# A ring of 24 row slots for the first expert layer, and a combination that fetches two row blocks a step

## The chip, the cores and the metric

The kernel runs on one core of a Trainium2 chip. Time is device microseconds (us) of the whole launch. TensorE multiplies matrices (PE in the profile), VectorE is DVE, ScalarE is ACT, GpSimd is POOL, and SyncE (SP) only issues transfers. Each engine works through a list of its own in order and waits on semaphores for the others. "DMA" is a transfer; an indirect one gathers or scatters rows by a list of indices, and is issued from POOL's list here.

## The reference

Input x is 8 batches of 512 tokens with 128 values. Four layers follow, each added to x and each behind a layer norm: a linear one with a cumulative sum, a mixture of experts, local attention, and the same mixture of experts again. The experts:

```python
xn = (x - mu) * rsqrt(var + EPS) * gamma + beta
probs = softmax(einsum('btd,ed->bte', xn, router_w) / TEMP)
w, idx = top_k(probs, 2)                 # 2 of E = 8 experts per token
h = silu(einsum('btd,edf->betf', xn, W1))
y = einsum('betf,efd->betd', h, W2)
out = einsum('bte,betd->btd', wdense, y) # the two chosen experts, weighted
return out + res
```

The attention has 16 heads of 8 values; a query sees itself and the 128 tokens before it.

## The kernel before, in words

**Tiles of an expert layer.** Tokens are sorted by expert, so that each tile of 128 row slots has one expert; there are 71 tiles. A router works out for each slot which token it holds (`idx`) and where each token's two results lie (`posi`). It does so in two halves of four batches: the tiles below FIRST = 25 need the first half alone, tile 25 and all later ones the second half too. The normalised rows lie in DRAM as `table`. POOL fetches the 128 rows of a tile into a slot of `xg` (L502), TensorE transposes them (L1180, `xbank`), ScalarE scales them (L973, L974), VectorE forms the low part of `xT` (L829), TensorE multiplies by W1 (L1198 to L1200), ScalarE applies silu (L980), TensorE multiplies by W2 (L1208), VectorE copies the result into one of eight slots of `ysb` (L825), and in the first layer SP stores it to `yslot` (L332). In the second layer POOL scatters it to `ytab` (L509).

**Steps.** `layer_pass` lets every engine go through the same steps s. In step s TensorE transposes tile s, multiplies tile s - 2 by W1 and tile s - 4 by W2; VectorE copies the result of tile s - 5 first and then makes `xT` of tile s. The product of tile i by W2 waits until the results up to tile i - 2 are copied. POOL fetches tile s + 3. It may do so when the tile four before it has been transposed, since `xg` has G = 4 slots. In the first layer steps 4 to 21 also hold the router of the second half (`r_step`), and steps 0 to 7 the linear layer of batches 4 to 7 (`a_step`), whose norms need a rsqrt guess from POOL (`pow_`, L465). Steps 24 to 35 each hold one of 12 memsets of POOL (L492) that zero the space `qz` for the attention.

**What lies beside the tiles.** From step BESIDE_AT = 44 on, when the first 40 tiles (all that batches 0 to 3 need) are through, `beside` adds other work of the first layer at the end of a step. Its own count starts at 0 in step 44. POOL gathers the results of batches 0 to 3 back from `yslot` (L522), eight gathers of 128 rows for a batch, one a step from count 2 on. Each waits until the tile under way (s - 3) has passed W1. VectorE adds them to x (`combine`, L846), batch b at counts 11 + 8b and 12 + 8b, when all eight have landed. Then come the fronts of batches 0 and 1, which prepare their attention: statistics on VectorE (L575 to L584), a rsqrt guess on POOL, which stands behind that step's fetch and gather, normalising on VectorE (L604), transposes and the products for q, k and v on TensorE (L1092, L1229 to L1241), a dump of q and k to DRAM and their stacks back into `qz` and `kst` by SP (L373). FRONT_AT = 12 sets where batch 0's front starts, batch 1's comes 8 counts later. When the pass is over, TensorE issues four warming products (L1356) and the scores of batch 0 (L1267, L1272), which wait for its stacks and alternate with reductions of VectorE (L889).

**The space that the change uses.** `pT` holds exponentials in the attention alone: 128 partitions by 3072 values, as much as 24 slots of 128.

## Time and profile before

| | us |
|---|---|
| median of 3 runs | 809.58 |
| lowest, highest | 806.76, 812.36 |
| the profiled execution | 813.83 |
| its span (first to last instruction) | 812.1 |
| busy: TensorE, VectorE, ScalarE, POOL | 664.5, 455.8, 421.8, 331.7 |
| first expert layer: tile 0's transpose to the last W2 product | 73.5 to 267.2 |
| second expert layer: the same | from 598.7 |

An engine's busy time is a sum over stages that are bound by different things, so it has to be read beside the timeline of the stretch in question. "idle before <-releaser" in a row tells what ended an engine's wait; "issue" there means that it waited for nothing that the profile shows.

### The profile page before, as it was taken

What the parts mean: (1) busy time and instruction counts of PE and PEld (TensorE: products, weight loads), DVE (VectorE), ACT (ScalarE), POOL (GpSimd) and SP (SyncE); (2) the same over time, 40 slices, a digit from 0 to 9 for tenths busy, and PEclk for the clock granted to TensorE, in tenths of its full rate; (3) what the DMA queues carried; (4) which work ended last, traced back from release to release, by engine and by line L of the source; (5) the groups of instructions that cost most, each with busy time, mean ns of one, the idle gap of its engine ahead of it and who ended that gap; (6) DMA issues with size and microseconds to landing.
All of it is one profiled execution on the core that took longest, in us unless ns stands there. A gap on an engine that the chain in (4) does not pass through costs nothing.

```text
span 812.1 us, 29237 instructions
## 1 busy us (share of the span) xinstructions
PE 664.5 (82%) x11190; PEld 516.6 (64%) x11190; DVE 455.8 (56%) x1700; ACT 421.8 (52%) x804; POOL 331.7 (41%) x352
## 2 busy tenths in 40 slices
PE   4942988999989788989898988779669799888890
PEld 2521686888878447566665656556448687777680
DVE  7866768522345666575666665573865842224334
ACT  3442375666655047464565657355548465555440
POOL 4303442585777101131212100110056677777771
PEclk9985799999999679899999999797878999999996
DMA  7500031222334301121120201010012111214425
GB/s 225 146 9 17 21 91 44 56 68 73 83 75 116 118 17 60 36 67 50 56 79 20 83 17 58 15 41 6 3 33 73 43 53 51 53 53 116 130 67 165
DMA packets 61029, 52.57 MB, mean 65 GB/s; under 512 B 9729, under 2 KB 54402, under 8 KB 60890
## 3 DMA queue, kind: packets, MB, share of 16 engines
q1 hardware_dynamic: 52034, 32.54, 13.6%
q0 software_dynamic: 8864, 18.17, 8.5%
q8 instruction: 96, 1.57, 0.8%
q14 instruction: 35, 0.29, 0.1%
HBM read 30.74 MB, written 19.92 MB: 62 GB/s over the span
## 4 chain that ended last, share of the span: by engine, by line
PE 47%; DVE 19%; issue 10%; POOL 7%; DMA 7%; ACT 4%; DVEq 4%; SPq 1%; PEld 1%; PEldq 0%; POOLq 0%; ACTq 0%
PE stbank L1208 10%; PE bank L1314 4%; DMA xg<-table,idx 4%; PE stbank L1198 3%; PE sbank L1272 3%; POOL ytab L509 3%; PE sbank L1267 3%; PE stbank L1298 3%; PE stbank L1200 2%; POOL xg L502 2%; DVE mx L889 2%; PE stbank L1199 2%; PE bank L1092 2%; DVE zr L604 2%; PE sbank L1180 1%
## 5 line engine op out<-in xcount | busy, mean ns | idle before, releaser
L502 POOL DMA_INDIRECT xg<-table,idx x142 | 139.1, 980 | 151.0 <-DVE sidx L815 87.5
L1208 PE MATMUL stbank<-wdn,g 128*128 x1136 | 166.6, 291 | 8.9 <-DVE ysb L825 7.6
L1208 PEld LDWEIGHTS stbank<-wdn,g 128*128 128x128 f32 x1136 | 141.6, 196 | 24.5 <-issue 11.7
L889 DVE TENSOR_REDUCE mx<-sbank 128x2 f32<-128x320 f32 (+1 forms) x256 | 116.4, 471 | 72.5 <-PE sbank L1272 67.7
L1033 ACT ACTIVATE pT<-stbank 128x1024 f32<-128x1024 f32 (+1 forms) x128 | 117.0, 916 | 77.0 <-PE stbank L1298 76.5
L973 ACT ACTIVATE xa<-sbank,be_s,ga_s 128x128 f32<-128x128 f32 x142 | 64.9, 457 | 132.2 <-PE sbank L1180 131.4
L1198 PE MATMUL stbank<-xT,wup 128*128 128x128 f16 x568 | 118.5, 229 | 3.9 <-issue 3.7
L1200 PE MATMUL stbank<-xT,wup 128*128 128x128 f16 x568 | 118.7, 229 | 0.0
L1199 PE MATMUL stbank<-xT,wup 128*128 128x128 f16 x568 | 116.7, 225 | 0.0
L522 POOL DMA_INDIRECT cg<-yslot,posi x64 | 61.5, 962 | 128.1 <-ACT pT L1033 114.3
L465 POOL TENSOR_TENSOR r<-ve,mhalf 128x4 f32<-128x4 f32 (+1 forms) x32 | 43.0, 1343 | 157.7 <-DVE ve L584 99.8
L980 ACT ACTIVATE g<-stbank 128x512 f32<-128x512 f32 x142 | 84.7, 597 | 22.9 <-PE stbank L1200 21.3
L829 DVE TENSOR_TENSOR xT<-xa,xT 128x128 f16<-128x128 f32 x142 | 41.3, 291 | 97.6 <-ACT xT L974 97.5
L1272 PE MATMUL sbank<-kst,qz 127*32 127x160 f16 (+1 forms) x2048 | 89.8, 249 | 1.0 <-issue 1.0
L825 DVE COPY ysb<-stbank 128x128 f32<-128x128 f32 x142 | 40.8, 288 | 77.6 <-PE stbank L1208 76.5
L1314 PE MATMUL bank<-pT,vp 128*32 128x256 f32 (+1 forms) x1024 | 79.1, 375 | 5.9 <-ACT ohl L1038 4.7
L509 POOL DMA_INDIRECT ytab<-ysb,sidx x71 | 71.1, 1001 | 25.4 <-issue 15.4
L1198 PEld LDWEIGHTS stbank<-xT,wup 128*128 x568 | 57.2, 101 | 17.2 <-issue 8.4
L1298 PE MATMUL stbank<-qz,kst 128*32 128x160 f16 (+4 forms) x2048 | 62.8, 233 | 3.5 <-issue 3.2
L974 ACT ACTIVATE xT<-sbank,be_s,ga_s 128x128 f16<-128x128 f32 x142 | 63.9, 450 | 0.0
L1200 PEld LDWEIGHTS stbank<-xT,wup 128*128 x568 | 56.9, 100 | 4.6 <-issue 0.8
L1199 PEld LDWEIGHTS stbank<-xT,wup 128*128 x568 | 57.7, 102 | 1.6 <-issue 0.3
(213 smaller groups left out, 1089.3 us busy)
## 6 DMA issues: line engine op xcount, KB each, us to landing
yslot<-ysb SPq DMA_DIRECT2D x71, 64.0 KB
table<-zr SPq DMA_DIRECT2D x16, 256.0 KB, 2.2
qz<-dumps SPq DMA_DIRECT2D x96, 32.0 KB
kst<-dumps SPq DMA_DIRECT2D x96, 32.0 KB
cg<-ytab SPq DMA_DIRECT2D x12, 256.0 KB, 3.8
xg<-table,idx POOLq DMA_INDIRECT x142
xs<-in_x SPq DMA_DIRECT2D x8, 256.0 KB, 4.8
qz<-in_w SPq DMA_DIRECT2D x1, 2048.0 KB, 9.2
```

The lines of the kernel that those rows point to most:

```text
L502: g.indirect_dma_start(xg[:, i % G, :], None, table if t >= FIRST else table[0:CHUNK, :], bass.IndirectOffsetOnAxis(ap=idx[:, t:t + 1], ax ...
L509: g.indirect_dma_start(ytab, bass.IndirectOffsetOnAxis(ap=sidx[:, t:t + 1], axis=0), ysb[:, i % RESULTS, :], None).then_inc(s_sc[i % RESUL ...
L889: ins = v.tensor_reduce(mx[:, qt, 4 * s + 2 * half:4 * s + 2 * half + 2], src, AX.X, ALU.max)
L980: a.activation(g32[:, i % 3, :], hbank[i % 2], ACT.Silu, scale=1.0 / WSCALE).then_inc(s_g32, 1)
L1033: a.activation(pT[:, i % 3, 0:4 * w].rearrange("p (g n) -> p g n", g=4), src, ACT.Exp, scale=SCALE).then_inc(s_e, 1)
L1198: mm(o, wh, xh, start=True, stop=False)
L1199: mm(o, wh, xl, start=False, stop=False)
L1200: ins = mm(o, wl, xh, start=False, stop=True)
L1208: ins = mm(ybank[i % 2], g32[:, i % 3, P * f:P * f + P], w[:, 0, P * f:P * f + P], start=(f == 0), stop=(f == FC - 1))
L1272: ins = mm(heads[r, g, 0:w], qz[0:P - 1, slot, 4 * s + 2 * half + g, P * qt + BLK * c:P * qt + BLK * c + BLK], kst[0:P - 1, slot, s, k0:k0 ...
L1298: ins = mm(o[r, BLK * c:BLK * c + n], kst[:, slot, s, P * kt + BLK * c:P * kt + BLK * c + BLK], qz[:, slot, 4 * s + g, P * kt + BLK * c:P ...
L1314: ins = mm(bank[0][32 * g:32 * g + 32, P * kt:P * kt + w], vp[:, b % 3, kt, VW * h:VW * h + 32], pT[:, i % 3, w * g:w * g + w], start=(kt ...
```

## The change

Five things change, all by constants and by the functions that say what stands in which step.

1. The ring has G = 24 slots, and its space is that of `pT`. In the first layer the fetches run ahead of the tiles: two a step in steps 1 to 7, tiles 18 to 24 in step 8, and from step 9 on tile s + 16. In the second layer the fetch stays at tile s + 3, and its first one waits for the attention's last product that reads `pT`.
2. The 12 memsets all stand in step 8, ahead of its fetches.
3. From count 2 on POOL issues two gathers a step instead of one, so a batch takes four steps.
4. The combination of batch b moves to counts 7 + 4b and 8 + 4b.
5. FRONT_AT becomes 8, so everything of the fronts of batches 0 and 1 stands four steps earlier.

```diff
--- before.py
+++ after.py
@@ -48,15 +48,17 @@
 KEPT = FULL + E
 LATE = TILES - FIRST
 WSCALE = 64.0
-G = 4
+G = 24
 RESULTS = 8
-AHEAD = G - 1
-ZERO_AT, ZEROS = 24, 12
+AHEAD, AHEAD_FIRST, SECOND_AT = 3, 16, 8
+ZEROS = 12
 GATHERS = 2 * TPB
+PER_STEP = 2
+BATCH_STEPS = GATHERS // PER_STEP
 BACK_AT = 2
 BESIDE_AT = KEPT + 4
 LOAD_EVERY = 6
-FRONT_AT = BACK_AT + GATHERS + 2
+FRONT_AT = BACK_AT + BATCH_STEPS + 2
 FRONT_EVERY = 8
 FRONT_STEPS = 14
 MAX_SPLIT = 3 * TPB
@@ -131,7 +133,7 @@
         idx = sb("idx", [P, TILES], U32); sidx = sb("sidx", [P, TILES], U32)
         eg3 = sb("eg3", [1, TILES - FULL, E]); egf = sb("egf", [1, TILES - FULL]); egc = sb("egc", [1, TILES - FULL])
         egi = sb("egi", [1, TILES - FULL], I32); eid = sb("eid", [1, TILES], I32)
-        xg = sb("xg", [P, G, D]); xa = sb("xa", [P, 2, P]); xT = sb("xT", [P, 3, 2 * P], F16)
+        xa = sb("xa", [P, 2, P]); xT = sb("xT", [P, 3, 2 * P], F16)
         g32 = sb("g32", [P, 3, H])
         ysb = sb("ysb", [P, RESULTS, D]); cg = sb("cg", [P, 2, TPB, 2, D])
 
@@ -140,6 +142,7 @@
         vp = sb("vp", [P, 3, TPB, VROW]); vsum = sb("vsum", [P, 3, 1]); zsum = sb("zsum", [P, 2]); bv_all = sb("bv_all", [P, 1])
         mx = sb("mx", [P, TPB, NH]); mT = sb("mT", [NH, SEQ], F16)
         pT = sb("pT", [P, 3, 4 * 256])
+        xg = pT[:].rearrange("p a n -> p (a n)").rearrange("p (g d) -> p g d", d=D)
         posb = key
 
         uT = ohl[:].rearrange("p k t n -> p (k t n)").bitcast(F32).rearrange("p (s n) -> p s n", s=SETS)
@@ -220,6 +223,14 @@
 
             return (TILES * layer + n, CHUNKS * layer + (n >= FIRST), n) if 0 <= n < TILES else (None, None, None)
 
+        def fetched_at(layer, s):
+
+            if layer:
+                return range(AHEAD + 1) if s == 0 else (s + AHEAD,)
+            if s < SECOND_AT:
+                return range(4) if s == 0 else range(2 * s + 2, 2 * s + 4)
+            return range(2 * SECOND_AT + 2, G + 1) if s == SECOND_AT else (s + AHEAD_FIRST,)
+
         def scattered(slot, end):
 
             return (end - 1 - slot) // RESULTS - (TILES - 1 - slot) // RESULTS
@@ -229,7 +240,7 @@
             return KEPT if b < BPC else TILES
 
         def gathered_back_at(s):
-            return s - BACK_AT if 0 <= s - BACK_AT < BPC * GATHERS else None
+            return range(PER_STEP * (s - BACK_AT), PER_STEP * (s - BACK_AT + 1)) if 0 <= s - BACK_AT < BPC * BATCH_STEPS else ()
 
         def loaded_back_at(s):
             b = (s - BACK_AT) // LOAD_EVERY
@@ -246,8 +257,8 @@
         def combined_at(layer, s):
             if layer:
                 return loaded_back_at(s - 3)
-            b = s - BACK_AT - GATHERS - 1
-            return b // GATHERS if b >= 0 and b % GATHERS == 0 and b // GATHERS < BPC else None
+            b = s - BACK_AT - BATCH_STEPS - 1
+            return b // BATCH_STEPS if b >= 0 and b % BATCH_STEPS == 0 and b // BATCH_STEPS < BPC else None
 
         def prepared_at(s):
             return [(b, s - FRONT_AT - FRONT_EVERY * b) for b in range(2) if 0 <= s - FRONT_AT - FRONT_EVERY * b < FRONT_STEPS]
@@ -483,17 +494,19 @@
                     pool.wait_ge(s_h, i + 1)
 
             def x_step(layer, s):
-                if layer == 0 and ZERO_AT <= s < ZERO_AT + ZEROS:
-
-                    if s == ZERO_AT:
-                        pool.wait_ge(s_wl, E)
+                if layer == 0 and s == SECOND_AT:
+
+                    pool.wait_ge(s_wl, E)
                     n = 3 * NH * SEQ // ZEROS
-                    z = qz[:].rearrange("p u h n -> p (u h n)")[:, n * (s - ZERO_AT):n * (s - ZERO_AT + 1)]
-                    g.memset(z.bitcast(F32), 0.0).then_inc(s_zero, 1)
-                for n in range(AHEAD + 1) if s == 0 else (s + AHEAD,):
+                    for k in range(ZEROS):
+                        z = qz[:].rearrange("p u h n -> p (u h n)")[:, n * k:n * k + n]
+                        g.memset(z.bitcast(F32), 0.0).then_inc(s_zero, 1)
+                for n in fetched_at(layer, s):
                     i, cc, t = layer_tile(layer, n)
                     if i is None:
                         continue
+                    if t == 0:
+                        wait(pool, s_pv, UNITS * B * layer)
                     if t in (0, FIRST):
                         pool.wait_ge(s_idx, cc + 1)
                         for k in range(BPC):
@@ -528,8 +541,7 @@
                     pow_(z_attn(b), 0, 0)
 
             def beside(layer, s):
-                m = gathered_back_at(s)
-                if layer == 0 and m is not None:
+                for m in gathered_back_at(s) if layer == 0 else ():
                     tile_under_way(layer, BESIDE_AT + s)
                     gather_back(m // GATHERS, m % GATHERS)
                 if layer == 0:
```

On POOL, this is the place where the first layer's gathers begin (`cg` is the space of the combination, L522 the gathers, L502 the fetches). Before:

```order
L492 MEMSET qz 128x1024
L502 DMA xg<-table,idx 128x128 [waits x_transposed] x12
L522 DMA cg<-yslot,posi 128x128 [waits y_stored4,y_stored3,y_stored5,y_stored2,y_stored6,y_stored1,y_stored7,y_stored0,h_psum]
L502 DMA xg<-table,idx 128x128 [waits x_transposed]
L522 DMA cg<-yslot,posi 128x128 [waits h_psum]
```

The same place in the changed kernel (the ring is named `pT` there), with what leads to it from the memsets on, and the last of its rows with the rsqrt guess of batch 0's front:

```order
L503 MEMSET qz 128x1024 x11
L515 DMA pT<-table,idx 128x128 x6
L515 DMA pT<-table,idx 128x128 [waits x_transposed]
L515 DMA pT<-table,idx 128x128 [waits table_rows_stored2,table_rows_stored3,table_rows_stored1,x_transposed,table_rows_stored0,slot_indices_ready]
L515 DMA pT<-table,idx 128x128 [waits x_transposed] x37
L535 DMA cg<-yslot,posi 128x128 [waits y_stored4,y_stored3,y_stored5,y_stored2,y_stored6,y_stored1,y_stored7,y_stored0,h_psum]
...
L535 DMA cg<-yslot,posi 128x128 [waits combined,h_psum]
L535 DMA cg<-yslot,posi 128x128 [waits h_psum]
L476 TENSOR_TENSOR r<-ve,mhalf 128x4 [waits variance_ready]
```

The memsets have left the fetches, 38 fetches (tiles 25 to 62) stand in a row behind the wait for the indices, and the guess stands behind 18 gathers and the fetch of the last tile.

On VectorE, this is the combination of batch 1 and the end of batch 0's norm. Before, the norm has its step to itself (L591 to L604):

```order
L825 COPY ysb<-stbank 128x128 [waits y_stored6,y_psum]
L829 TENSOR_TENSOR xT<-xa,xT 128x128 [waits x_high]
L591 TENSOR_TENSOR newt<-r 128x4 [waits rsqrt_guess]
L593 TENSOR_TENSOR newt<-newt,ve 128x4
```

In the changed kernel the combination of batch 1 stands ahead of it in the same step:

```order
L837 COPY ysb<-stbank 128x128 [waits y_stored2,y_psum]
L841 TENSOR_TENSOR xT<-xa,xT 128x128 [waits x_high]
L858 SCALAR_TENSOR_TENSOR xs<-cg,wk,xs 128x128 [waits y_gathered1,residual_scaled]
L858 SCALAR_TENSOR_TENSOR xs<-cg,wk,xs 128x128 x3
L603 TENSOR_TENSOR newt<-r 128x4 [waits rsqrt_guess]
```

The step is number 59 before and 55 now.

## Rows read from the trace of the kernel before

**Rows 1.** The page, part 1: busy time of the engines.
```profile
PE 664.5 (82%) x11190; PEld 516.6 (64%) x11190; DVE 455.8 (56%) x1700; ACT 421.8 (52%) x804; POOL 331.7 (41%) x352
```

**Rows 2.** The chain of waits, 214 to 238 us: start, duration, what.
```profile
216.52 1.01 POOL cg L522
...
229.18 0.95 POOL cg L522
...
230.16 1.05 POOL r L465
```

**Rows 3.** The timeline of POOL, 152 to 268 us: start, duration, instruction, idle before.
```profile
152.64 0.95 POOL L502 DMA_INDIRECT xg<-table,idx  x1 [6.40 <-DVE sidx L815]
...
154.84 0.97 POOL L492 MEMSET qz<- 128x1024 f32 x1
...
182.64 0.94 POOL L502 DMA_INDIRECT xg<-table,idx  x1 [0.30 <-issue]
183.89 0.94 POOL L502 DMA_INDIRECT xg<-table,idx  x1 [0.30 <-issue]
...
199.03 0.94 POOL L522 DMA_INDIRECT cg<-yslot,posi  x1 [0.30 <-issue]
...
267.62 0.95 POOL L522 DMA_INDIRECT cg<-yslot,posi  x1 [0.30 <-issue]
```

**Rows 4.** The timeline of TensorE: transposes of tiles 18, 37, 46, 57 and 70.
```profile
139.11 0.31 PE L1180 MATMUL sbank<-ident,xg 128*128 128x128 f32 x1
...
181.04 0.27 PE L1180 MATMUL sbank<-ident,xg 128*128 128x128 f32 x1
...
199.15 0.27 PE L1180 MATMUL sbank<-ident,xg 128*128 128x128 f32 x1
...
221.43 0.27 PE L1180 MATMUL sbank<-ident,xg 128*128 128x128 f32 x1
...
256.60 0.29 PE L1180 MATMUL sbank<-ident,xg 128*128 128x128 f32 x1
```

**Rows 5.** The timeline of TensorE: W2 of tiles 57 and 70, the attention's start.
```profile
233.82 1.95 PE L1208 MATMUL stbank<-wdn,g 128*128 x8 [2.09 <-DVE ysb L825]
...
266.01 1.15 PE L1208 MATMUL stbank<-wdn,g 128*128 x8 [1.06 <-DVE ysb L825]
...
269.18 1.02 PE L1356 MATMUL stbank<-mband,ident 128*128 128x512 f16 x4
272.26 0.41 PE L1267 MATMUL sbank<-mlower,ident 128*32 128x256 f16 x4 [2.06 <-DMA kst<-dumps]
```

**Rows 6.** The timeline of POOL, 111 to 114 us.
```profile
111.52 1.09 POOL L502 DMA_INDIRECT xg<-table,idx  x1 [0.19 <-issue]
112.92 0.94 POOL L502 DMA_INDIRECT xg<-table,idx  x1 [0.30 <-issue]
```

**Rows 7.** The timeline of VectorE: a norm, combinations of batches 0 and 3.
```profile
113.16 1.11 DVE L604 TENSOR_SCALAR zr<-xs,mv,rr 128x128 f32<-128x128 f32 x4
...
220.22 1.14 DVE L846 SCALAR_TENSOR_TENSOR xs<-cg,wk,xs 128x128 f32<-128x128 f32 x4 [1.64 <-DMA cg<-yslot,posi]
...
270.35 2.35 DVE L846 SCALAR_TENSOR_TENSOR xs<-cg,wk,xs 128x128 f32<-128x128 f32 x8 [2.86 <-DMA cg<-yslot,posi]
```

**Rows 8.** The timeline of POOL in the second expert layer.
```profile
592.45 1.02 POOL L502 DMA_INDIRECT xg<-table,idx  x1 [48.22 <-DVE sidx L815]
...
638.81 1.09 POOL L509 DMA_INDIRECT ytab<-ysb,sidx  x1 [3.28 <-DVE ysb L825]
...
793.90 0.97 POOL L509 DMA_INDIRECT ytab<-ysb,sidx  x1 [0.30 <-issue]
```

**Rows 9.** The chain of waits: the attention's last product that reads pT.
```profile
589.17 0.57 PE bank L1314 x8
```

**Rows 10.** Windows: length, busy us of PE, PEld, DVE, ACT, POOL, clock, DMA.
```profile
230.00:240.00 10.00, 7.91 (x65) 7.11 (x65) 3.15 (x14) 3.89 (x10) 7.94 (x9) 0.83 0.26 66
...
275.00:290.00 15.00, 12.53 (x296) 6.57 (x292) 11.98 (x33) 1.78 (x2) 0.56 (x1) 0.55 0.17 50
```

## The prediction

> **What bounds the kernel now.** I read the page first: TensorE is busy 82% of the span [rows 1], but the share is a mean over stages, so the next view was the chain of waits around the end of the first expert layer. Up to 216.5 us it runs through TensorE. From there to 230.2 us it runs through POOL alone, one gather after the other, then through POOL's rsqrt guess and VectorE to a TensorE product at 233.82 us [rows 2, 5]. So POOL's queue is already the limit where the combination lies beside the tiles.
>
> The timeline of POOL gives the price of an order: rows are fetched at 182.64 and 183.89 us, 1.25 us apart (0.94 busy, 0.30 between), with nothing to wait for [rows 3]. The 24 orders from 199.03 to 229.18 us take 30.15 us, 1.256 each [rows 2, 3]. The timeline of TensorE gives a step (one tile): the transposes of tiles 37 and 57 start at 181.04 and 221.43 us, 2.02 us a step [rows 4]. Steps that hold a fetch and a gather cost POOL 2.51 us against TensorE's 2.02, and that lag is what the chain shows.
>
> The end of the layer is the third place. The last tile's product is at 266.01 us, the attention's first scores start at 272.26 after an idle 2.06 us for the stacks of batch 0 [rows 5].
>
> **The change, part by part.** I write step s for the turn in which tile s is transposed.
>
> *More fetches early, zeroing in one block.* Steps 1 to 7 issue two fetches each (1.25 us more before the rsqrt guesses of the second router), step 8 issues 12 memsets (0.97 us each, 11.6 us [rows 3]) and seven fetches. In the trace POOL's first fetch behind the fourth guess of that router is at 111.52 us [rows 6]. The block thus ends near 111.5 + 11.6 + 8.8 = 132 us. Tile 18, the first one behind the memsets, is wanted at 139.11 us [rows 4]. The guesses come at most 1.25 us later, and VectorE takes each up only after its next statistics. Cost 0, covered by VectorE's own router work; without this cover 1.25 us a guess.
>
> *Tile 25.* Its rows need the second router's indices. POOL waits for them now, too: its fetch starts at 152.64 us after a wait for sidx [rows 3]. The longer ring moves nothing here. POOL reaches the wait earlier and leaves it at the same time. This is the anchor of the sum.
>
> *Fetches until step 45.* Before, memsets stood between them (154.84 us [rows 3]) and then the ring of four held them to TensorE. Now 37 fetches (tiles 25 to 61) run at 1.25 us: 152.64 + 46.3 = 198.9 us. Step 46 begins there with the fetch of tile 62. TensorE is at tile 46 at 199.15 us [rows 4]; no slot is short, since tile 62 needs tile 38 gone.
>
> *Steps 46 to 54, one fetch and two gathers each.* That is 3.77 us of POOL beside 2.02 us of TensorE. A gather still waits for the tile under way, so it can't start before step 46. With two gathers a step the last of batch 0's eight is order 11 after 198.9 (start 212.7), the last of batch 1's order 23: 198.9 + 23 x 1.256 = 227.8 us. From such an order's start to VectorE's first use took 3.70 us (216.52 to 220.22 [rows 2, 7]), for the last batch 2.73 us (267.62 to 270.35 [rows 3, 7]). I take 3.70, since the former has fetches queued around it as here, and keep 2.73 for the low end.
>
> The Trainium skill, DMA: Bandwidth & Descriptors, section "Anatomy of one DMA", fits 2.0 us plus bytes over 436 GB/s for a transfer. For 64 KB behind an order of 1.01 us that is 3.2 us instead of 3.7; by that the sum would be 0.5 us smaller.
>
> *VectorE now asks sooner.* Batch 0's combination moves from step 55 to 51, batch 1's from step 63 to 55. Step 51 starts five steps behind 199.15, at 209.2 us, so VectorE stands at the gathers near 210.5 and gets them at 212.7 + 3.7 = 216.4: a first wait of 6 us, where there were 1.64 [rows 7]. Step 55 starts at 217.3 us without this wait, near 222.5 with it. VectorE is there at 224 and gets batch 1's rows at 227.8 + 3.7 = 231.5 us: a second wait of 7.5 us. Behind each of them on VectorE stand the result copy and the xT part of the next tiles, and TensorE waits for these after about one step of slack.
>
> *The rsqrt guess of batch 0.* It stands behind step 54's fetch and two gathers: 227.8 + 3 x 1.256 + 0.95 = 232.5, ready at 233.6 us. VectorE then needs what it needed before: guess ready 231.2, TensorE's product at 233.82 [rows 2, 5], 2.6 us. So TensorE goes on at 236.2 us. Before, that product was tile 57's. Now it is tile 53's, because the same front stands four steps earlier in the program.
>
> *From there to the attention.* Before, 233.82 to 272.26 is 38.44 us [rows 5]. Now the anchor is 236.2 - 233.8 = 2.4 us later, and four more tiles follow it, 4 x 2.02 = 8.1 us. Off come the 2.06 us for the stacks, which are loaded four steps earlier, and some of the tail. From tile 70's transpose at 256.60 to the end of the warming products at 270.2 are 13.6 us [rows 4, 5] with about 11 us of products in them (five down products at 1.0, three up at 0.7, batch 1's front 2.8, the warming ones 1.0). Of the 2.6 us of waits I take off 1.8, since the front's last links then lie beside tiles. Sum: 2.4 + 8.1 - 2.1 - 1.8 = **6.6 us later**.
>
> *The second layer.* There AHEAD stays 3 and the order of fetches and scatters is the same. From 638.81 us on POOL issues without a pause, 1.28 us each, to its last scatter at 793.90 [rows 8], so a longer ring adds nothing. The start of that stretch is released by VectorE's copy, so an earlier fetch before it is worth nothing, either. The new wait for the attention's last product is over when the index is ready: that product starts at 589.17, the fetch at 592.45 us [rows 8, 9]. Cost 0, covered by the index; without it at most the part of the product behind it, 0.6 us. The gathers of batches 4 to 7 in the attention don't move.
>
> The profiled execution took 813.83 us (span 812.1), so it would take 820.4. The median of the runs shown, 809.58, is 4.25 lower; with the same 6.6 us it gives **816.2 us**.
>
> **Rivals.**
>
> *POOL keeps up, faster.* The change is worth what it says if batch 1's gathers are in by the time VectorE reaches step 55, 218.5 us. Then the present lag goes (TensorE's idle 2.09 us before 233.82 and 0.8 us of slow products behind it: 2.9 us [rows 5]), with it the 2.1 and 1.8 us of the tail and about 1.5 us of the same lag in front of batch 1: -8.3 us, 801.3 us. It needs 13 us less over 60 orders, 1.03 us an order. For it: the memset at 154.84 us follows its fetch with no gap [rows 3]. Against: fetches and gathers in a row keep the 0.30 us with nothing to wait for [rows 3]. Chance 0.10.
>
> *Given back by the clock, no change.* The first 16 units of scores run at half clock (0.55 granted, 1.2 GHz for most of it [rows 10]), after a stretch of little work. If TensorE comes to them without the idle 2.06 us and stays at 2.4 GHz, each unit saves up to half of its products, 0.3 us, 4.7 us in all: +1.9 us, 811.5. Against: VectorE's reductions fill 11.98 of 15 us there [rows 10], which leaves less than 3 us. Cases between -3 and +3 us: chance 0.15.
>
> *Slower than the sum.* After the idle 2.09 us before 233.82 us the clock fell: 0.83 granted over 230 to 240 us, and the eight products took 1.95 instead of 1.15 us [rows 5, 10]. The second wait idles TensorE for over 8 us, which may make the next steps dearer by 1 to 3 us beyond what the same stretch already shows. A few more conflicts on the way come on top: +9 to +12 us, 818.6 to 821.6. Chance 0.17.
>
> In the trace four normalising instructions of VectorE at 113.16 us take 1.11 us beside a fetch of POOL at 112.92 [rows 6, 7], so they do not hold each other up; where the memsets now lie, these VectorE instructions run beside memsets for the first time, at most four of 0.97 us: 3.9 us. This, too, would end in the case above, 820.1. The Trainium skill, SBUF — State Buffer, section "Who interferes with whom", says that GpSimd and a two-port instruction of VectorE exclude each other for a whole instruction, which is a rule against this change; by it the 3.9 us would be paid, less what VectorE waits anyway.
>
> **How the numbers follow.** Forecast 0.58, its own range +3.5 to +9.5 us (low: a landing of 2.73 us and all 2.6 us of the tail; high: nothing of the tail's waits), slower 0.17, no change 0.15, POOL keeps up 0.10. Low 808 and high 821.5 leave out most of the fast case and a little at the top, with 1.5 us for the spread of the runs. A measurement here can tell about 1% (8.1 us) from nothing. The forecast of 6.6 lies below that: of its 0.58 I put 0.15 above 8.1, with the slower case 0.32. The fast case sits on the border, 0.08 beyond. The rest, 0.60, is within 1%.
>
> **What would show it.** On POOL a row of 37 fetches at 1.25 us from 152.6 to 199 us, then three orders a step without a pause, the 16th gather at 227.8 +- 1. On VectorE two waits for cg of some 6 and 7.5 us, at 210 and 224 us, where one of 1.64 stood. TensorE idle before 236 us, then no wait for kst before the scores, which start at 278.9 us instead of 272.26. POOL free near 251 instead of 268.6 us. From 640 us on the same pace as before. The prediction is wrong if orders come closer than 1.2 us, if VectorE's two waits are short, or if the first scores start before 275 us.

## The result, and the profile after

| | before | after |
|---|---|---|
| median (runs) | 809.33 (4) | 828.47 (4) |
| lowest, highest | 806.76, 812.36 | 823.21, 832.57 |
| the profiled execution, its span | 813.83, 812.1 | 823.21, 821.5 |

The change makes the kernel slower: ratio 1.0219, interval 1.017 to 1.0267, some 18 us (whether it is by more than 2% stays open). The prediction said 816.2 us with a range up to 821.5, so the direction of the sum was right and its size was not. The profiled execution of before is 4.5 us above its median, that of after is the shortest of its four, 5.3 below. That is why the two traces differ by 9.4 us and the medians by 19.

The page, part 1, of after, to be read beside [rows 1]:

```profile
PE 650.2 (79%) x11190; PEld 509.4 (62%) x11190; DVE 466.0 (57%) x1700; ACT 420.1 (51%) x804; POOL 330.0 (40%) x352
```

TensorE was busy 14 us less for the same instructions (its clock was higher in places), yet the span is longer, so what was added is waiting. In the functions concerned, line numbers of after are 11 to 13 higher than those of before: L604 is now L616, L1208 is L1220. The timeline of POOL, after (start, duration, instruction, idle before):

```profile
109.40 1.66 POOL L476 TENSOR_TENSOR r<-ve,mhalf 128x8 f32<-128x8 f32 x1 [2.02 <-DVE ve L596]
111.03 10.76 POOL L503 MEMSET qz<- 128x1024 f32 x12
121.97 1.02 POOL L515 DMA_INDIRECT pT<-table,idx  x1 [0.18 <-issue]
...
165.28 0.95 POOL L515 DMA_INDIRECT pT<-table,idx  x1 [34.80 <-DVE sidx L827]
...
240.33 0.94 POOL L535 DMA_INDIRECT cg<-yslot,posi  x1 [0.30 <-issue]
...
245.05 1.04 POOL L476 TENSOR_TENSOR r<-ve,mhalf 128x4 f32<-128x4 f32 x1
```

Tile 25's fetch stood at 152.64 us [rows 3] and is at 165.28 now. From there on POOL does what the prediction says, 12.6 us later: the 16th gather, forecast for 227.8, starts at 240.33. Why tile 25's indices are late is in the timeline of VectorE:

```profile
110.34 11.60 DVE L616 TENSOR_SCALAR zr<-xs,mv,rr 128x128 f32<-128x128 f32 x4
121.86 0.27 DVE L837 COPY ysb<-stbank 128x128 f32<-128x128 f32 x1
...
123.48 1.10 DVE L616 TENSOR_SCALAR zr<-xs,mv,rr 128x128 f32<-128x128 f32 x4
...
227.88 1.14 DVE L858 SCALAR_TENSOR_TENSOR xs<-cg,wk,xs 128x128 f32<-128x128 f32 x4 [4.53 <-DMA cg<-yslot,posi]
...
242.97 1.14 DVE L858 SCALAR_TENSOR_TENSOR xs<-cg,wk,xs 128x128 f32<-128x128 f32 x4 [7.72 <-DMA cg<-yslot,posi]
...
246.13 0.16 DVE L603 TENSOR_TENSOR newt<-r 128x4 f32<-128x4 f32 x1 [2.02 <-POOL r L476]
```

The four normalising instructions of the linear layer took 1.11 us [rows 7], the first group now takes 11.60 us, until 121.94. The memsets run from 111.03 to 121.79. The next group, with no memset beside it, is at 1.10 again. In the trace of before no norm of VectorE starts between 114 and 232 us, and the memsets all lie in there. The timeline of TensorE:

```profile
121.99 1.12 PE L1104 MATMUL bank<-ident,zr 128*128 128x128 f32 x4 [11.11 <-DVE zr L616]
...
248.72 1.65 PE L1220 MATMUL stbank<-wdn,g 128*128 x6 [10.51 <-DVE ysb L837]
...
288.19 1.04 PE L1368 MATMUL stbank<-mband,ident 128*128 128x512 f16 x4 [0.39 <-DVE ysb L837]
289.16 0.29 PE L1279 MATMUL sbank<-mlower,ident 128*32 128x256 f16 x4
```

TensorE waits 11.11 us for those values. The 10.51 us end with VectorE's result copy; that copy stands on VectorE behind its waits for batch 1's gathers (7.72 us) and the guess of batch 0 (2.02 us). In front of the scores the wait of 2.06 us for the stacks [rows 5] is gone. Stretches of after (length; busy time of TensorE, weight loads, VectorE, ScalarE, POOL; granted clock; DMA share; GB/s):

```profile
108.00:124.00 16.00, 4.89 (x38) 4.45 (x38) 15.25 (x30) 3.36 (x9) 14.12 (x15) 0.68 0.07 17
240.00:255.00 15.00, 6.28 (x35) 5.87 (x36) 5.44 (x22) 1.98 (x5) 11.65 (x13) 0.66 0.28 63
289.00:303.00 14.00, 11.05 (x342) 5.67 (x340) 12.10 (x30) 0.82 (x2) 0.00 (x0) 1.00 0.22 67
524.00:576.00 52.00, 39.87 (x985) 29.15 (x978) 30.19 (x126) 27.00 (x43) 6.54 (x4) 0.87 0.08 24
```

and of before:

```profile
108.00:124.00 16.00, 15.34 (x166) 14.72 (x166) 9.93 (x49) 14.07 (x34) 8.41 (x8) 1.00 0.30 80
272.00:289.00 17.00, 14.80 (x340) 7.80 (x340) 13.53 (x37) 0.78 (x2) 0.00 (x0) 0.51 0.20 60
512.00:567.00 55.00, 43.58 (x990) 32.61 (x986) 30.41 (x126) 27.37 (x43) 6.55 (x4) 0.78 0.08 22
```

From 108 to 124 us TensorE was busy 15.3 us and is now busy 4.9. That is the loss. The score stage (first scores to POOL's next guess) ran at a granted clock of 0.51, near 1.2 GHz, and now runs at 1.00, 2.4 GHz: 272.26 to 289.44 us before, 289.16 to 303.81 now, 2.5 us shorter. Another 2.9 us come back in the last window, a batch of the attention (54.8 us from one addition to x to the next before, 51.9 now), where the execution of before was at 0.78 and that of after at 0.87. Why the clock differed there isn't shown.

### The profile page after: what moved, and what is told of

Same layout as the page of the kernel before. It is cut to its first block, busy times and chain, and to the rows that moved or that the text cites. A ratio compares the mean times of both kernels' runs of the same rounds, so it can differ in the third digit from the quotient of the medians.

```text
span 821.5 us, 29237 instructions
## 1 busy us (share of the span) xinstructions
PE 650.2 (79%) x11190; PEld 509.4 (62%) x11190; DVE 466.0 (57%) x1700; ACT 420.1 (51%) x804; POOL 330.0 (40%) x352
## 4 chain that ended last, share of the span: by engine, by line
PE 46%; DVE 22%; issue 10%; DMA 7%; POOL 6%; DVEq 4%; ACT 4%; PEld 1%; SPq 0%; PEldq 0%; POOLq 0%; ACTq 0%
PE stbank L1220 10%; DMA pT<-table,idx 4%; PE bank L1326 4%; PE stbank L1210 3%; DVE zr L616 3%; PE sbank L1284 3%; POOL ytab L522 3%; PE sbank L1279 3%; PE stbank L1310 2%; PE stbank L1212 2%; DVE mx L901 2%; PE stbank L1211 2%; PE bank L1104 2%; DVE xs L858 2%; POOL pT L515 2%
## 5 line engine op out<-in xcount | busy, mean ns | idle before, releaser
L515 POOL DMA_INDIRECT pT<-table,idx x142 | 137.5, 968 | 154.8 <-DVE sidx L827 113.9
L1220 PE MATMUL stbank<-wdn,g 128*128 x1136 | 166.3, 291 | 20.0 <-DVE ysb L837 18.1
L1220 PEld LDWEIGHTS stbank<-wdn,g 128*128 128x128 f32 x1136 | 142.0, 197 | 33.7 <-issue 22.2
L476 POOL TENSOR_TENSOR r<-ve,mhalf 128x4 f32<-128x4 f32 (+1 forms) x32 | 43.5, 1359 | 165.4 <-DVE ve L596 92.0
L1284 PE MATMUL sbank<-kst,qz 127*32 127x160 f16 (+1 forms) x2048 | 84.7, 234 | 0.9 <-issue 0.9
L1326 PE MATMUL bank<-pT,vp 128*32 128x256 f32 (+1 forms) x1024 | 77.3, 369 | 7.2 <-ACT ohl L1050 6.1
L522 POOL DMA_INDIRECT ytab<-ysb,sidx x71 | 71.6, 1008 | 28.3 <-issue 14.2
```

What stands on the lines that cost most here:

```text
L515: g.indirect_dma_start(xg[:, i % G, :], None, table if t >= FIRST else table[0:CHUNK, :], bass.IndirectOffsetOnAxis(ap=idx[:, t:t + 1], ax ...
L522: g.indirect_dma_start(ytab, bass.IndirectOffsetOnAxis(ap=sidx[:, t:t + 1], axis=0), ysb[:, i % RESULTS, :], None).then_inc(s_sc[i % RESUL ...
L1220: ins = mm(ybank[i % 2], g32[:, i % 3, P * f:P * f + P], w[:, 0, P * f:P * f + P], start=(f == 0), stop=(f == FC - 1))
L1284: ins = mm(heads[r, g, 0:w], qz[0:P - 1, slot, 4 * s + 2 * half + g, P * qt + BLK * c:P * qt + BLK * c + BLK], kst[0:P - 1, slot, s, k0:k0 ...
L1326: ins = mm(bank[0][32 * g:32 * g + 32, P * kt:P * kt + w], vp[:, b % 3, kt, VW * h:VW * h + 32], pT[:, i % 3, w * g:w * g + w], start=(kt ...
```

## A common zero for the runs

Executions differ by up to 5 us before the parts under test matter: from 20 to 60 us TensorE was busy 25.8 us in ring_alone and 29.2 in ring_and_warming, whose code is the same there. So the table counts from the start of the last rsqrt guess of the second router, **T0**. That is this row of POOL in the kernel before, the 109.40 row in after:

```profile
109.68 1.66 POOL L465 TENSOR_TENSOR r<-ve,mhalf 128x8 f32<-128x8 f32 x1 [3.73 <-DVE ve L584]
```

| kernel (us after T0) | T0 | tile 25's fetch | first scores | second layer's first fetch | median us, ratio |
|---|---|---|---|---|---|
| before | 109.68 | 43.0 | 162.6 | 482.8 | 809 to 811 |
| the change | 109.40 | 55.9 | 179.8 | 492.3 | 828.47, 1.022 |
| change_again | 113.00 | 56.6 | 181.0 | 493.3 | 826.73, 1.019 |
| block_alone | 109.78 | 56.0 | 174.4 | 491.9 | 822.06, 1.014 |
| gap_between | 113.12 | 43.5 | 170.8 | 483.3 | 816.29, 1.008 |
| paced_zeroing | 109.76 | 46.3 | 170.6 | 483.7 | 814.12, 1.006 |
| pairs_alone | 111.66 | 43.3 | 175.8 | 488.0 | 818.32, 1.008 |
| ring_and_block | 112.28 | 55.9 | 169.8 | 489.7 | 813.91, 1.003 |
| ring_alone | 108.13 | 43.3 | 155.0 | 469.1 | 799.88, 0.989 |
| gathers_first | 112.35 | 42.9 | 156.2 | 472.8 | 801.28, 0.989 |
| longer_warming | 109.42 | 43.0 | 162.6 | 479.1 | 807.09, 0.995 |
| ring_and_warming | 112.17 | 43.0 | 155.6 | 473.1 | 802.64, 0.988 |

Medians are over 4 to 10 runs, and the ratios are against runs of before on the same chip. The runs stand on several chips, so a difference of two medians and of two ratios can be apart by some 3 us; where both are given below, they bound the cost. The column of tile 25's fetch says it at once: 55.9 to 56.6 where the block of memsets is unbroken, 42.9 to 43.5 elsewhere, with one exception explained below.

## The experiments

**block_alone.** The kernel before, with the memsets as one block in step 8 instead of one a step from 24.

```diff
-                if layer == 0 and ZERO_AT <= s < ZERO_AT + ZEROS:
+                if layer == 0 and s == 8:
...
+                    for k in range(ZEROS):
+                        z = qz[:].rearrange("p u h n -> p (u h n)")[:, n * k:n * k + n]
+                        g.memset(z.bitcast(F32), 0.0).then_inc(s_zero, 1)
```

> The kernel before, with one part of the change alone: its 12 memsets stand in a block in step 8 instead of one a step in steps 24 to 35. Theory A (the block of memsets holds VectorE up): the normalising instructions of VectorE beside it take 11 to 12 us instead of 1.1, tile 25's fetch starts near 164 us instead of 152.6, the first scores near 284 us instead of 272.3, and the time is 10 to 12 us above the kernel before. Rival B (VectorE was held up by the fetches two a step, the block is harmless): normalising takes 1.1 us, tile 25's fetch starts at 152 to 153 us, the time is within 3 us of before.

Measured: 822.06 us (815.52 to 822.8), ratio 1.0141 (1.0074 to 1.0209). VectorE's timeline:

```profile
110.71 11.60 DVE L604 TENSOR_SCALAR zr<-xs,mv,rr 128x128 f32<-128x128 f32 x4
```

The block alone has the 11.60 us and a fetch of tile 25 that is 13.1 us late after T0. Of that 11.8 us are left at the scores, and 11.8 in the median (822.06 for 810.24). Theory A holds. The ring and the pairs have no part in it.

**gap_between.** The change, with each memset waiting for the one before it.

```diff
                     for k in range(ZEROS):
+                        wait(pool, s_zero, k)
                         z = qz[:].rearrange("p u h n -> p (u h n)")[:, n * k:n * k + n]
```

> The changed kernel, but each of the 12 memsets in the block waits for the one before it, so that POOL leaves a gap between two. Theory A1 (memsets in an unbroken row keep the port, a gap lets VectorE in): four normalising instructions wait for at most one memset each, 4 x 0.97 = 3.9 us, tile 25's fetch starts near 157 us instead of 165.3, time 7 to 9 us below the changed kernel. Theory A2 (VectorE loses to every memset anyway, gap or not): normalising takes 11.6 us or more, tile 25's fetch at 165 us or later, time as the changed kernel.

Measured: 816.29 us (811.13 to 818.04), ratio 1.0075 (1.0042 to 1.0108). POOL, then VectorE:

```profile
114.75 12.13 POOL L504 MEMSET qz<- 128x1024 f32 x12
```

```profile
114.06 1.78 DVE L617 TENSOR_SCALAR zr<-xs,mv,rr 128x128 f32<-128x128 f32 x4
115.76 0.27 DVE L838 COPY ysb<-stbank 128x128 f32<-128x128 f32 x1
115.96 0.27 DVE L842 TENSOR_TENSOR xT<-xa,xT 128x128 f16<-128x128 f32 x1
...
117.27 1.66 DVE L617 TENSOR_SCALAR zr<-xs,mv,rr 128x128 f32<-128x128 f32 x4
```

The same 12 memsets, 1.4 us longer in all, lie beside the same instructions of VectorE, and these take 1.78 and 1.66 us instead of 11.60. So it is neither the memsets' place nor their sum that costs, but that nothing separates them. Theory A1 holds, and the hold costs less than it said: tile 25's fetch is 0.5 us later after T0, not 4. The change's ratio of 1.0219 (1.0185 when it was measured again) falls to 1.0075, 9 to 12 us.

The rows show one thing more: only some instructions of VectorE are held. The second memset starts at 115.75 us and takes 0.98 us. The copy at 115.76 and the TENSOR_TENSOR at 115.96 run beside it in 0.27 us each, their usual time; what waited was TENSOR_SCALAR, the form of the normalising. The same holds in the kernel before, where the memset of 154.84 us [rows 3] had this beside it:

```profile
154.96 0.29 DVE L829 TENSOR_TENSOR xT<-xa,xT 128x128 f16<-128x128 f32 x1 [0.66 <-ACT xT L974]
```

An xT of 196.05 us, with no memset near, takes 0.29 us too. So the place of the memsets in steps 24 to 35, where VectorE has copies and xT to do, was a harmless one.

**paced_zeroing.** The memsets stand behind step 8's fetches, each waits until another tile has been transposed.

```diff
+PACED_FROM = 11
...
+                if layer == 0 and s == SECOND_AT:
+                    n = 3 * NH * SEQ // ZEROS
+                    for k in range(ZEROS):
+                        pool.wait_ge(s_xp, PACED_FROM + k)
...
```

> The changed kernel with its 12 memsets behind the fetches of step 8, each waiting for one more transposed tile (11 to 22), so that no two stand in a row. If the prediction's other steps hold, this is the time that it forecast without the lock: tile 25's fetch at 152.6 to 154 us, the 16th gather starts at 227.8, tile 53's W2 product at 236.2 us, the first scores at 277 us (the changed kernel's 289.2 less 12.6), time 10 to 13 us below the changed kernel, 815 to 818 us. Rival: the combination's waits are a result of the late router alone; then they shrink with it, and the first scores start before 270 us.

Measured: 814.12 us (810.48 to 819.32), ratio 1.006 (1.0026 to 1.0093). The groups of norms near the memsets take 1.10 to 1.11 us. The time is just under the range expected, and every place is 3.4 us later than expected: tile 25's fetch at 156.10, the 16th gather at 231.20, tile 53's product at 239.57, the scores at 280.36. The fetch is 3.4 us late after T0, too, which the memsets don't explain (the first starts at 120 us). The stretch 108 to 116 us of this kernel, then of before:

```profile
108.00:116.00 8.00, 7.95 (x49) 7.86 (x50) 5.76 (x33) 5.34 (x14) 5.13 (x5) 0.53 0.33 80
```

```profile
108.00:116.00 8.00, 7.34 (x74) 6.90 (x75) 6.20 (x35) 6.32 (x17) 4.63 (x4) 1.00 0.28 72
```

TensorE did 49 products here at a clock of 0.53, 74 at 1.00 before. In ring_alone, whose code is the same up to there, the clock was 1.00 and tile 25 was at 43.3. So that delay belongs to the execution, and not to the edit. What remains of the change without the lock: +0.6%, 4 to 5 us, with TensorE's wait for the pairs at tile 53:

```profile
239.57 1.64 PE L1222 MATMUL stbank<-wdn,g 128*128 x6 [10.42 <-DVE ysb L839]
```

**gathers_first.** As paced_zeroing, but no row fetches in steps 46 to 54 (the ring holds 16 tiles of lead, 8 remain), and batches 2 and 3 gathered one a step again.

```diff
+HOLD = 46, 55
+GATHER_COUNTS = [2 + m // 2 if m < 16 else 10 + (m - 16) for m in range(32)]
+COMBINE_COUNTS = 7, 11, 19, 27
...
+            return (s + AHEAD_FIRST,) if s < HOLD[0] else () if s < HOLD[1] else (s + AHEAD_FIRST - (HOLD[1] - HOLD[0]),)
```

> As the kernel with paced memsets, but in steps 46 to 54 POOL fetches no tiles (they are 16 ahead by then) and goes on with tile 62 in step 55, eight ahead; batches 2 and 3 are gathered one a step again and combined at counts 19 and 27. If POOL's orders ahead of batch 1's last gather set VectorE's wait, that gather starts near 217.7 us instead of 227.8, VectorE's two waits for gathered rows shrink from 4.5 and 7.7 us to about 1 and 3, the first scores start near 267 us, time 8 to 11 us below the paced kernel. Rival: the waits come from the landing of the transfers and not from POOL's orders; then they stay within 2 us of what they were.

Measured: 801.28 us (798.26 to 806.31), ratio 0.9885 (0.9832 to 0.9939). VectorE's two combinations:

```profile
213.05 1.13 DVE L864 SCALAR_TENSOR_TENSOR xs<-cg,wk,xs 128x128 f32<-128x128 f32 x4
...
223.11 1.14 DVE L864 SCALAR_TENSOR_TENSOR xs<-cg,wk,xs 128x128 f32<-128x128 f32 x4 [1.67 <-DMA cg<-yslot,posi]
```

Waits of 0 and 1.67 us, where the change has 4.53 and 7.72. So POOL's orders set these waits, and 16 paired gathers cost VectorE 1.67 us of waiting if no fetches stand between them. The time falls by 13 to 14 us against paced_zeroing, more than the 8 to 11 expected; two parts are undone at once here (the fetches between, the pairs of batches 2 and 3), and the run doesn't divide the gain between them.

**ring_alone.** As paced_zeroing, with the gathers of the combination one a step and the fronts where they were.

```diff
-PER_STEP = 2
+PER_STEP = 1
```

> The ring of 24 with its early fetches, the zeroing paced one tile per transpose behind step 8's fetches (so that VectorE is not held), but the combination's gathers one a step and the first fronts as in the kernel before. Theory A (what is left of the slowdown once the zeroing is paced, +4 to +5 us, is TensorE's wait for POOL's paired gathers, 10.4 us at tile 53, taken back in part by work already done): that wait is gone here. No wait over 3 us on POOL's or a gather's account between 200 and 265 us, the last gather lands before 262 us, the scores start between 269 and 275 us (272.26 before), with the 3 us or so that a low clock after 108 us costs when it comes. Time 806 to 812 us, the same as before within 0.5%. Theory B (the ring itself costs: row fetches far ahead, 24 rows of buffers, a longer start): scores at 278 or later and 814 us or more, as with paced zeroing and pairs (814.12).

Measured: 799.88 us (798.58 to 804.65), ratio 0.9891 (0.9836 to 0.9946). That is better than either theory had it: 9 us by the ratio, 11 by the medians. I had taken the ring alone for no gain. POOL and TensorE:

```profile
221.50 1.06 POOL L537 DMA_INDIRECT cg<-yslot,posi  x1 [0.32 <-issue]
222.87 0.94 POOL L537 DMA_INDIRECT cg<-yslot,posi  x1 [0.30 <-issue]
224.11 0.94 POOL L537 DMA_INDIRECT cg<-yslot,posi  x1 [0.30 <-issue]
225.26 1.04 POOL L477 TENSOR_TENSOR r<-ve,mhalf 128x4 f32<-128x4 f32 x1 [0.21 <-DVE ve L595]
```

```profile
228.15 0.27 PE L1194 MATMUL sbank<-ident,pT 128*128 128x128 f32 x1
...
230.50 0.27 PE L1194 MATMUL sbank<-ident,pT 128*128 128x128 f32 x1
```

POOL's fetches are over with step 54 (217.64 us), so the later gathers come 1.24 to 1.37 us apart with no fetch between. T0 is 1.6 us earlier here than in the kernel before, which has to be taken off the differences that follow. Batch 0's guess starts at 225.26 (230.16 before [rows 2]), and TensorE goes from tile 61's transpose to tile 62's in 2.35 us. In the kernel before it took 5.71:

```profile
230.71 0.27 PE L1180 MATMUL sbank<-ident,xg 128*128 128x128 f32 x1
...
236.42 0.42 PE L1180 MATMUL sbank<-ident,xg 128*128 128x128 f32 x1
```

Tile 70's transpose is at 247.75 us, 256.60 before [rows 4], 7.3 us earlier after T0. The first gather is 1.4 us later after T0 than before (198.90 and 199.03 us [rows 3]). So the gain is made in the steps that hold gathers, and not by where the memsets stand. Against paced_zeroing, where the pairs are the one difference, the pairs cost 14 us on top of the ring.

**pairs_alone.** The change, with the ring, the fetches and the memsets as before.

```diff
-G = 24
+G = 4
...
-            if s < SECOND_AT:
-                return range(4) if s == 0 else range(2 * s + 2, 2 * s + 4)
-            return range(2 * SECOND_AT + 2, G + 1) if s == SECOND_AT else (s + AHEAD_FIRST,)
+            return range(AHEAD + 1) if s == 0 else (s + AHEAD,)
```

> The kernel before (ring of 4, fetches 3 tiles ahead, zeroing one memset a step from step 24) with two gathers a step for the combination and the first two fronts earlier. Theory A (POOL's queue orders a step's work at 0.95 us for a row fetch and 1.25 us for each gather, 3.4 to 3.7 us a step against 2.1 for a tile on TensorE, and only the ring's lead hides that): with 3 tiles of lead TensorE waits for the row fetches through the 16 steps: some 16 x 1.4 less the lead of 3 tiles (6 us), +15 to +20 us at tile 57, of which the early fronts fill a part: scores start at 280 to 290 us, time 816 to 828 us. Theory B (the pair's cost is hidden anyway, the ring is idle weight): scores at 272 to 277 us and 806 to 813 us.

Measured: 818.32 us (811.55 to 822.99), ratio 1.0084 (1.0046 to 1.0122). TensorE now waits for the fetched rows, six times between 215 and 247 us, 5.9 us in all; three of them, and the front's wait:

```profile
215.23 0.33 PE L1188 MATMUL sbank<-ident,xg 128*128 128x128 f32 x1 [1.57 <-DMA xg<-table,idx]
...
221.97 0.33 PE L1188 MATMUL sbank<-ident,xg 128*128 128x128 f32 x1 [0.50 <-DMA xg<-table,idx]
...
229.15 0.33 PE L1188 MATMUL sbank<-ident,xg 128*128 128x128 f32 x1 [1.20 <-DMA xg<-table,idx]
...
237.46 2.07 PE L1216 MATMUL stbank<-wdn,g 128*128 x8 [2.85 <-DVE ysb L833]
```

The fetch and two gathers of a step cost 3.75 us, and a lead of three tiles can't cover that. The scores start 13.2 us late after T0. Scores and time lie in Theory A's ranges; tile 57's transpose is 9.9 us late after T0, where it had 15 to 20.

**ring_and_block.** The change with one gather a step, the block kept.

```diff
-PER_STEP = 2
+PER_STEP = 1
```

> The change with one thing undone: one gather a step and the first fronts as before, the ring of 24 and the unbroken block of 12 memsets kept. Theory A (the parts add up: the ring alone gave 10 to 11 us, the block alone cost 11 to 12 us, and the pairs make the rest of the 19 us): tile 25's fetch at 162 to 166 us, scores at 275 to 279 us, time 809 to 814 us, the kernel before within 0.5%, and so the pairs cost 14 to 17 us of the change (826 to 828 us). Theory B (the lead of 16 tiles soaks up the block's 11 us, as none of the fetches waits long): scores at 268 us or before, 803 us or less. Theory C (with the block the ring's gain is lost too, since the fetches ahead are the ones held back): 816 us or more.

Measured: 813.91 us (809.59 to 823.26), ratio 1.0027 (0.9996 to 1.0058). The profiled execution is the longest of the ten, so its rows serve for places only: tile 25's fetch at 55.9, the scores at 169.8 after T0. The block costs 11 us by the ratios (1.0027 and 0.9891) and 14 by the medians (799.88) on top of the ring, and the pairs make the other 13 to 15 us of the change. Theory A's parts add up within that: the time is in its range, and tile 25's fetch (168.2 us) and the scores (282.1) lie 2 to 3 us above theirs with a T0 that is 2.6 us late.

**longer_warming.** The kernel before, with 12 warming products instead of 4.

```diff
-            for a2 in range(4):
-                mm(stbank[:, a2, :], ident16[:], mband[:]...
+            for a2 in range(12):
+                mm(stbank[:, a2 % 4, :], ident16[:], mband[:]...
```

> The kernel before with 12 warming products instead of 4 ahead of the first layer's scores, so that TensorE has work in the 2.06 us in which it waits for kst. Theory A (the idle stretch ahead of the scores lets the clock fall to 0.50 for the score stage, and that is what the changed kernel, which starts its scores with no wait, gives back): scores start at 272 to 273 us, the clock granted from 276 to 288 us is 1.00, the stage takes 13.5 instead of 16.5 us, and the time falls by 2 to 3.5 us (806 to 808 us). Theory B (the clock in that stage has another cause, such as the load of scores itself): clock 0.50 as before, time unchanged or up to 0.5 us longer.

Measured: 807.09 us (802.94 to 815.57), ratio 0.9949 (0.9923 to 0.9976). TensorE, and the stretch 276 to 288 us:

```profile
269.07 2.75 PE L1356 MATMUL stbank<-mband,ident 128*128 128x512 f16 x12
...
272.02 0.29 PE L1267 MATMUL sbank<-mlower,ident 128*32 128x256 f16 x4 [0.20 <-DMA kst<-dumps]
```

```profile
276.00:288.00 12.00, 8.65 (x276) 4.44 (x268) 10.78 (x32) 1.87 (x2) 0.86 (x1) 1.00 0.18 53
```

The scores start when they did, the clock in their stage is 1.00 instead of 0.50, the stage takes 15.1 us for 17.2 (13.5 for 16.5 expected), and the next addition to x (L904) follows them by 55.6 instead of 61.8 us. Of these 6.2 us 3.7 are left at the second layer and 3.5 in the median (4.1 by the ratio). Theory A holds.

**ring_and_warming.** ring_alone with the 12 warming products.

```diff
-            for a2 in range(4):
+            for a2 in range(12):
```

> The ring alone, paced zeroing and single gathers, with 12 warming products instead of 4 ahead of the scores. Theory A (the stretch of 2.35 us in which TensorE waits for kst is what puts its clock at 0.50 for the score stage here too): clock 1.00 from 266 to 276 us, a score stage shorter by 2.5 to 3 us, time 796 to 798.5 us, the fastest of all. Theory B (what follows the stage is bound by another clock fall or by VectorE, so the gain is lost): 799 to 801 us.

Measured: 802.64 us (798.67 to 806.55), ratio 0.9881 (0.9838 to 0.9924), not to be told from ring_alone; Theory A's 796 to 798.5 us was missed. The stage was 2.5 us shorter (14.65 for 17.18 us) and ran at 1.00, though 1.06 us of the wait for the stacks were left. Later in the attention, one batch took 2.6 us more than in ring_alone (38.3 for 35.7 us), with this stretch at its end:

```profile
428.00:437.00 9.00, 7.05 (x28) 4.46 (x26) 3.36 (x14) 1.90 (x3) 2.49 (x3) 0.68 0.09 26
```

And T0 was 4.0 us later. Whether the two gains add stays open.

**change_again.** The change itself once more, with no edit, beside ring_alone, pairs_alone and longer_warming.

> The change once more, unaltered, beside the others on this chip. The block of 12 memsets holds VectorE's normalization for 10.8 to 11.8 us, tile 53's W2 product waits 10 to 11 us, scores start at 288 to 292 us. 822 to 830 us, ratio 1.015 to 1.025; with the low clock in the stretch of the TensorE waits the span is at the long end.

Measured: 826.73 us (822.08 to 828.44), ratio 1.0185 (1.0126 to 1.0244). The profiled execution took 828.09 us, 4.9 more than the first one. POOL:

```profile
113.00 1.66 POOL L476 TENSOR_TENSOR r<-ve,mhalf 128x8 f32<-128x8 f32 x1 [2.46 <-DVE ve L596]
114.63 10.76 POOL L503 MEMSET qz<- 128x1024 f32 x12
```

T0 is 3.6 us later, the block as long as in the first one; the scores start at 293.97 us, 2 us above the range expected, since T0 is late. The stretch behind it, 124 to 140 us, of this execution and of the first:

```profile
124.00:140.00 16.00, 14.40 (x126) 14.30 (x127) 7.50 (x28) 10.36 (x23) 8.06 (x9) 0.72 0.31 80
```

```profile
124.00:140.00 16.00, 14.57 (x172) 14.27 (x172) 8.02 (x33) 13.37 (x29) 4.96 (x6) 0.89 0.27 75
```

Behind the idle stretch 126 products at a clock of 0.72 here, 172 at 0.89 there, in part since the block ends 3.6 us later. Of the 1.2 us by which the scores are later after T0 (181.0 and 179.8), 0.7 are there at tile 25's fetch. That the clock behind the hold makes them is likely and not shown.

## Why the prediction was wrong

**The step that failed** is *More fetches early, zeroing in one block*: "Cost 0, covered by VectorE's own router work". It cost 13 us at tile 25 (55.9 for 43.0 after T0) and 9 to 14 us of time: 11 to 12 in block_alone, 9 to 12 against gap_between, 10 to 14 against paced_zeroing, 11 to 14 between ring_and_block and ring_alone. I looked at when POOL would be through (forecast 132 us, measured 130.5) and whether tile 18 would be in time. It was. What the block does to VectorE while it runs, I met only in the rival *Slower than the sum*, and bounded it there by four memsets, one for each of the four instructions: 3.9 us. One instruction of VectorE waited 11.0 us, for all twelve. The nearest row was a memset that followed a fetch without a gap [rows 3], never two memsets in a row, so no row of before bounded a run of them. The upper bound should have been the whole run, 11.6 us.

The Trainium skill, SBUF — State Buffer, section "Who interferes with whom", gives an exclusive lock on the port pair that VectorE and GpSimd share. The traces agree with that rule (a normalising instruction stood still beside the memsets, 11.0 us for 0.34), and it spoke against this change; that the hold is one of ports, no run here shows by itself. Where the traces go further is the time: the hold outlasted an instruction's end (10.76 us over 12 memsets, 0.9 us apart) as long as the next one stood ready, and a semaphore wait between two memsets was enough to let VectorE in (1.78 us).

**The anchor at tile 25.** "POOL reaches the wait earlier and leaves it at the same time" holds as far as POOL is concerned. The indices it waits for come from VectorE, and the block had moved them.

**Fetches until step 45; steps 46 to 54.** Right: from tile 25's fetch to the 16th gather 75.16 us forecast, 75.05 measured (75.15 in gap_between). Landing and VectorE's waits: 6 and 7.5 forecast, 4.53 and 7.72 measured. The guess was ready at 246.09, tile 53's product at 248.72: forecast 233.6 and 236.2, plus 12.5.

**From there to the attention.** 42.7 us forecast, 40.4 measured in the change, 43.8 in gap_between, 40.8 in paced_zeroing. Each of these links of the sum lies within 2.3 us.

**The range.** The bounds +3.5 and +9.5 us don't follow from the terms named with them: 6.6 less 0.97 and 0.8 is 4.8, and 6.6 plus 1.8 is 8.4. The measured 18 us lie outside either way.

**The clock.** The rival *Given back by the clock* came true beside the forecast, not in its place. The scores without a wait before them ran at 1.00. The five profiled executions with all gathers paired (no wait for the stacks) took 312.2 to 313.1 us from the first scores to the second layer's fetch, before 320.2. I had said that VectorE's reductions leave less than 3 us of the 4.7: the stage itself gave 2.5, and longer_warming shows by itself that filling the wait brings the clock to 1.00. The rest isn't attributed: the kernels without the pairs took 314.1 to 319.9 us, also those that ran their score stage at 1.00.

**POOL keeps up.** This rival priced the lag of the kernel before at 8.3 us and put the time without it at 801.3. The change doesn't reach it, but gathers_first (801.28) and ring_alone (799.88) do, and by another way than the rival said: their orders stay 1.25 us apart instead of 1.03, and what goes is the fetches among the gathers. In ring_alone the scores are 7.6 us earlier after T0 although the wait for the stacks, which the rival counted as gone, is still there (2.35 us). That 801.3 us came so close is luck.

**The second layer.** Cost 0 forecast. From its first fetch to the start of the last scatter it took 201.4 us before [rows 8] and 201.7 after (601.71 to 803.42). It began 9.3 us late and the kernel ends 9.4 us late.

So with the block's hold taken away the sum was good: +6.6 us forecast, +4 (paced_zeroing) to +6 us (gap_between) measured. That it agrees so well is in part luck. In the trace of gap_between the scores are 8.2 us late after T0, and 7.7 us of that are back by the second layer, a stretch for which the sum took no change; the rest of the median's +6 us is spread between executions. And of the parts, the ring gives 9 to 11 us, the pairs on top of it cost about 14, the block 9 to 14. The best kernels found are ring_alone, gathers_first and ring_and_warming, 1.1 to 1.2% below before and not to be told apart.

## What to carry to other kernels

When work is moved to an idle stretch of one engine, ask what the other engines do in that stretch, not only whether the moved work is done in time; bound an unmeasured conflict by the whole run of the moved instructions. Zero on GpSimd in single pieces with a wait between them, or where VectorE has only instructions that aren't held. And a longer lead helps a queue only if its place in the queue is then left free: here it paid to fetch early and gather singly, and the same lead was spent again by two gathers a step.

## What the runs showed of the hardware

- 12 memsets of GpSimd in a row (128 x 1024 f32, 10.76 us) held a VectorE normalisation (TENSOR_SCALAR, 128 x 128 f32) for 11.0 us; with a semaphore wait between them four such instructions took 1.66 to 1.78 us, alone 1.11.
- A TENSOR_TENSOR and a copy out of `stbank` beside a memset took their usual 0.27 to 0.29 us (gap_between, before).
- Issues of indirect transfers held the norms little: groups of four took 1.11 us beside them, and the longest single norm beside such an issue in the kernel before took 0.57 us, 0.34 being usual.
- With 1.95 to 2.38 us of waiting ahead of the scores (before, block_alone, ring_alone, ring_and_block), TensorE's granted clock in their stage was 0.51 to 0.54; with products in place of that wait (1.06 us at most left, in ring_and_warming) it was 1.00.
